# The mask matmul of the self-attention scores in fp32r instead of bf16, in a decoder layer on one core

## What is computed

```python
scores = jnp.einsum('bhqd,bhkd->bhqk', q, k) * scale
scores = scores + _alibi_bias_causal(l, scores.dtype)[None]   # -inf above the diagonal
attn = jax.nn.softmax(scores, axis=-1)
out = jnp.einsum('bhqk,bhkd->bhqd', attn, v)
```

## Time and profile before

| | us |
|---|---|
| median of 3 runs | 2784.67 |
| lowest and highest run | 2781.45, 2797.6 |
| the profiled execution: device time | 2791.88 |
| its span, first to last instruction | 2790.1 |
| mean granted TensorE clock (share of full) | 0.954 |
| PE busy | 2495.2 (89%) |
| PEld busy | 2048.2 (73%) |
| DVE busy | 1714.9 (61%) |
| ACT busy | 1403.3 (50%) |
| POOL busy | 714.5 (26%) |

### The profile page before, as it was taken

The page is one execution under the profiler, slowest core; times in us unless marked ns, Lnnn a source line. Parts: engine busy times, 40 slices in busy tenths (PEclk is TensorE's granted clock), DMA queues, the critical chain, the costliest instruction groups (busy, mean ns, idle before and its releaser), DMA issues.

```text
span 2790.1 us, 70718 instructions
## 1 busy us (share of the span) xinstructions
PE 2495.2 (89%) x23737; PEld 2048.2 (73%) x23864; DVE 1714.9 (61%) x3714; ACT 1403.3 (50%) x3067; POOL 714.5 (26%) x1359
## 2 busy tenths in 40 slices
PE   3789999999999999999999999999999999999985
PEld 2577777777777777777777777777777777777774
DVE  3365666665666666666666566666666666656652
ACT  2245555555555545555555555555455555455542
POOL 2112222222222222222222222222222222222221
PEclk8799999999999999999999999999999999999996
DMA  3466556566556556556656655655665665665541
GB/s 74 63 89 90 88 88 96 84 90 93 82 85 96 91 83 96 84 87 96 90 83 93 92 87 87 96 89 85 96 88 81 93 95 85 92 87 87 90 76 21
DMA packets 162889, 240.65 MB, mean 86 GB/s; under 512 B 21790, under 2 KB 86030, under 8 KB 159766
## 3 DMA queue, kind: packets, MB, share of 16 engines
q1 hardware_dynamic: 161304, 239.99, 57.2%
q10 hardware_dynamic: 1536, 0.01, 0.0%
HBM read 53.12 MB, written 33.55 MB: 31 GB/s over the span
## 4 chain that ended last, share of the span: by engine, by line
PE 57%; DMA 24%; DVE 6%; SPq 4%; issue 4%; ACT 4%; ACTq 1%; POOL 0%; DVEq 0%; POOLq 0%
DMA q_stack<-q_nat 12%; PE ps_misc L474 10%; DMA ctx_in<-in_ctx 9%; PE ps_misc L488 9%; PE ps_max L540 4%; SPq L394 4%; PE ps_score L585 3%; PE ps_score L572 3%; PE ps_max L553 3%; PE ps_attend L600 3%; PE ps_max L530 3%; PE ps_score L574 3%; PE ps_score L576 3%; PE ps_misc L630 2%; PE ps_max L536 2%
## 5 line engine op out<-in xcount | busy, mean ns | idle before, releaser
L901 DVE TENSOR_REDUCE neg_max_s<-ps_max 128x2 f32<-128x512 f32 (+1 forms) x768 | 483.1, 682 | 111.3 <-PE ps_max L530 73.0
L750 ACT ACTIVATE probs<-ps_score 128x384 f32<-128x384 f32 x1024 | 470.0, 492 | 141.3 <-PE ps_score L576 135.4
L757 ACT ACTIVATE xprobs<-ps_score 120x512 f32<-120x512 f32 x512 | 295.5, 599 | 244.4 <-PE ps_score L585 237.1
L1018 POOL TENSOR_SCALAR ve_LN<-mv_LN 128x2 f32<-128x2 f32 x192 | 36.8, 191 | 1342.7 <-DVE mv_LN L923 1342.7
L574 PE MATMUL ps_score<-q_stack,k_stack 97*128 97x256 f32 x1024 | 378.1, 369 | 0.0
L909 DVE TENSOR_REDUCE neg_max_x<-ps_max 128x4 f32<-128x480 f32 x512 | 314.2, 651 | 70.3 <-PE ps_max L553 70.3
L572 PE MATMUL ps_score<-mask_k,ident_b 128*128 128x256 bf16 x1024 | 290.9, 284 | 22.6 <-DMA q_stack<-neg_max_t_s 15.0
L576 PE MATMUL ps_score<-q_stack,k_stack 97*128 97x256 f32 x1024 | 291.1, 284 | 0.0
L1044 POOL TENSOR_TENSOR res<-res,chain_n 128x512 f32<-128x512 f32 x64 | 82.4, 1288 | 605.2 <-ACT chain_n L795 605.2
L585 PE MATMUL ps_score<-xq_stack,xk_stack 97*120 97x256 f32 x1024 | 227.2, 314 | 3.5 <-DMA xq_stack<-neg_max_t_x 2.8
L574 PEld LDWEIGHTS ps_score<-q_stack,k_stack 97*128 97x128 f32 x1024 | 206.6, 202 | 1.5
(11 more groups left out here) (153 smaller groups left out, 6026.9 us busy)
## 6 DMA issues: line engine op xcount, KB each, us to landing
k_stack<-k_nat SPq DMA_DIRECT2D x192, 256.0 KB, 6.9
q_stack<-q_nat SPq DMA_DIRECT2D x192, 256.0 KB, 7.2
xq_stack<-q_nat SPq DMA_DIRECT2D x192, 256.0 KB, 6.0
xk_stack<-scr_xk SPq DMA_DIRECT2D x192, 128.0 KB, 3.7
x_in<-in_x SPq DMA_DIRECT2D x64, 256.0 KB, 3.2
scr_xk<-k_nat SPq DMA_DIRECT2D x32, 512.0 KB, 6.8
out_y<-res SPq DMA_DIRECT2D x64, 256.0 KB, 2.2
ctx_in<-in_ctx SPq DMA_DIRECT2D x32, 240.0 KB, 7.9
```

The lines of the kernel that those rows point to most:

```text
L750: act.activation(probs[:, h % 8, :], bank_of("SCORE", i, b, h)[:, P:4 * P], ACT.Exp)\
L757: act.activation(xprobs[0:C, at:at + 2, :], blocks(bank_of("XSCORE", i, b, u))[0:C], ACT.Exp).then_inc(sem("xprobs_ready"), 1)
L901: dve.tensor_reduce(o, ins, AX.X, ALU.max, negate=True).then_inc(sem("max_taken"), 1)
```

## The change

The mask tile `mask_k` is now made in fp32. ACT copies it and the fp32 identity into two new tiles of type fp32r, `mask_r` and `ident_r`, in the prologue, and the mask matmul of the scores uses these two. The masks of MAX stay in bf16. PE's first instruction now waits for these copies too.

```diff
-        mask_k = sb("mask_k", [P, 2, P], BF16)
+        mask_k = sb("mask_k", [P, 2, P])
+        mask_r = sb("mask_r", [P, 2, P], F32R)
+        ident_r = sb("ident_r", [P, P], F32R)
...
         def _(pe):
-            pe.wait_ge(sem("consts"), 4)
+            pe.wait_ge(sem("consts"), 6)
             pe.wait_ge(sem("w_loaded"), 16 * (len(PREP) + 1))
...
-                pe.matmul(bk[:, P:3 * P], ident_b[:, :], mask_k[:, :, :].rearrange("p a b -> p (a b)"),
+                pe.matmul(bk[:, P:3 * P], ident_r[:, :], mask_r[:, :, :].rearrange("p a b -> p (a b)"),
                           start=True, stop=False, skip_group_check=True)
...
             act.wait_ge(sem("consts"), 4)
+            act.activation(mask_r[:, :, :], mask_k[:, :, :], ACT.Copy).then_inc(sem("consts"), 1)
+            act.activation(ident_r[:, :], ident[:, :], ACT.Copy).then_inc(sem("consts"), 1)
```

## The result

The changed kernel takes 2807.93 us (median of 6 runs, 2802.72 to 2814.95), the kernel before 2790.32 us in the runs beside it. The ratio is 1.0067, 95% interval 1.0045 to 1.0088: 18 us slower, inside the 1% that I called no change. The profiled execution has a span of 2800.9 us and a mean granted clock of 0.957, practically that of before (0.954). That execution is the fastest of the six: device time 2802.72 us, only 10.8 us above the profiled execution of before (2791.88).

What follows compares the result with a forecast made beforehand. The prediction took PE, 57% of the chain, as the bound: 21 us of dearer weight loads on the path, +0.6 prologue, -10 clock, about +12 on 2784.67, so 2797 us; 8-in-10 range 2765 to 2828.

Runs made afterwards that it cites:

- e1_path: Kernel before, with the fp32r mask only for heads 0 to 8 of odd sequences and 9 to 15 of even ones; ratio 1.0298, 2870.46 us.
- f4_path_fill_q: e1_path plus four extra bf16 matmuls of 512 columns before MAX 0 of the even sequences; ratio 1.0068 to the kernel before.
- g2: Changed kernel with the context load issued ahead of the stacking of the maxima and of XQ; ratio 1.0136 to the kernel before, 2828.30 us.
- g1: Kernel before (bf16 mask) with the context load issued ahead of the stacking of the maxima and of XQ; ratio 1.0282, 2869.43 us.

## What to carry to other kernels

A narrow-type matmul that stands first in a group isn't only cheap itself. Behind a neighbour with a short stream or narrow tiles a part of the first weight load shows, and here it was less for the bf16 load (97 ns) than for the fp32r one (195 ns); its own stream then hides the longer load that follows. So keep it first and keep it narrow. Before pricing an edit of a few tenths of a microsecond, look at which waits of PE are followed by half the clock: work added in front of such a wait can be a gain, and the same work elsewhere can cost several times its own length (e1_path: 82 us for some 16). When an ablation's parts don't add up to the whole, compare the granted clock before anything else, and repeat the comparison with the waits filled.

## What the hardware showed that I hadn't expected

- Four matmuls of 512 columns per pair that nothing needs, put into a 2.0 us wait, made the kernel 0.5% faster, and took 2.2% off another (e1_path to f4_path_fill_q).
- The same edit is +0.7% in one order of DMA issues and -1.4% in another (g2 against g1).
- fp32 transposes of 128 columns pace at 0.11 us, and a 195 ns weight load behind them costs 0.01 more than a 97 ns one, while behind four bf16 matmuls of 120 columns it costs 0.07 and behind tiles of 32 columns 0.10.
- With the clock at full from start to end of the loop (1.00 against 0.97) the kernel gained no more than with 0.98: the time went into a wait for another buffer.
